# A residual block of two 3x3 convolutions: four operations of the inner planes change places on VectorE and ScalarE

## The chip, the cores and the metric

The kernel runs on one core of a Trainium2 chip. The metric is the device time in microseconds. Before the change the median of 3 runs is 612.59 us (612.04 to 614.04). A core has a matrix engine (TensorE, PE in the rows; its weight loads are PEld), VectorE (DVE), ScalarE (ACT), GpSimd (POOL) and SyncE (SP), each with a queue of its own that runs in order.

## The reference

The input x is 32 images of 64 channels, 56 x 56, in float32; w1 and w2 are 64 x 64 x 3 x 3.

```python
def _conv3x3(x, w, stride=1):
    return jax.lax.conv_general_dilated(x, w, window_strides=(stride, stride), padding=((1, 1), (1, 1)), ...)
def _bn(x, gamma, beta, mean, var):
    inv = gamma * jax.lax.rsqrt(var + EPS)
    return x * inv[None, :, None, None] + (beta - mean * inv)[None, :, None, None]
identity = x
out = jax.nn.relu(_bn(_conv3x3(x, w1, stride=1), g1, b1, m1, v1))
out = _bn(_conv3x3(out, w2, stride=1), g2, b2, m2, v2)
return jax.nn.relu(out + identity)
```

## The kernel before, in words

**Layout.** An image is split into four planes by the parity of row and column. The 128 partitions are 64 channels times the row parity; the column parity makes two planes per partition, "even" and "odd", of 28 rows by 28 columns.

**Transform.** Along a row each convolution of three taps is done for two neighbouring columns at once with four products instead of six: two "inner" ones, on the sum and on the difference of two planes, and two "outer" ones, on differences with a shift. The inner products go to the PSUM banks SUM_T1 and SUM_T2, the outer ones to EVEN and ODD. In between, a *join* on VectorE writes EVEN and ODD from SUM_T1 plus and minus SUM_T2, of which ScalarE has made two copies with the bias, z (*copy_sum*, L562 and L563). The outer products are added onto that. PSUM is used whole: two halves of an image (14 or 15 row pairs), each with its four banks, by both convolutions in turn.

**Precision.** Each transformed plane t goes to TensorE as hi plus lo: hi is t rounded (ScalarE, *high_x*, *high_hidden*), lo is t minus hi (VectorE, *split_x*, *split_hidden*). A product is three matmul passes, hi by w_hi, hi by w_lo and lo by w_hi, with two matmuls each for the two row offsets, so 12 for the two inner products of a half and 12 for the outer ones. An image takes 96.

**Names.** *sum_hidden*, *difference_hidden* (L427, L433) make the inner planes t_inner of conv 2 from `hidden`; *outer_hidden* (L441) makes t_outer. ti_hi and ti_lo are the rounded t_inner and its rest, h_hi and h_lo those of t_outer. There is one buffer of ti_hi and ti_lo. *residual* (L543) puts half of the input's inner planes into SUM_T1 and SUM_T2, so that conv 2's inner products add onto the identity. *relu_hidden* (L568) writes `hidden` from EVEN and ODD, *relu_out* (L591) writes out_sb, which SyncE stores.

**Steps.** All engines run the same steps s, written out by hand, in a loop of four steps a turn with some steps ahead and behind. In step s TensorE does: conv 1's inner products of image s and conv 2's outer products of image s-2, for half 0 and then for half 1 (48 matmuls); then conv 2's inner products of image s-1 and conv 1's outer products of image s, for half 0 and then half 1 (48 matmuls). The order on each engine is the order of the code; semaphores count the finished pieces. What matters here:

- join(1, s, 0) overwrites EVEN and ODD of half 0, and waits until relu_out(s-2, 0) has read them. relu_out(s-2, 0) waits for conv 2's outer products of half 0.
- join(2, s-2, 1) waits for relu_hidden(s-1, 1), and so does sum_hidden(s-1). TensorE's inner products of conv 1, half 1, wait for that join.
- high_hidden("inner", s-1) waits for both t_inner planes, split_hidden("inner", s-1) for ti_hi, and TensorE's inner products of conv 2 for ti_lo and for residual of their half.
- residual(s-1, 0) waits for join(1, s, 0), which has read SUM_T1 of that half.
- Step 0 and 1 have no relu_out or join of conv 2; the step after the last image is written apart, half by half.

```python
def join(conv, n, half, before):
    dve.wait_ge(z_ready[conv], 2 * n + half + 1)
    dve.wait_ge(inner[conv], 2 * (2 * n + half) + 2)
    wait(dve, *((hidden_ready if before[0] == 1 else out_ready), 2 * before[1] + half + 1))
```

Of the kernel before, what the change touches and what calls it, by code (L numbers as in the profile page):

```python
# [24 lines left out]
def residual_block(nc, x, w1, w2, params, out):  # L25
# [17 lines left out]
    with ExitStack() as ctx:  # L43
# [100 lines left out]
        def wait(eng, semaphore, value):  # L144

            if isinstance(value, int) and value <= 0:
                return
            eng.wait_ge(semaphore, value)
# [12 lines left out]
        def is_step(s, number):  # L161

            return isinstance(s, int) and s == number

        def there_is(s, image):

            return not isinstance(s, int) or 0 <= image < N
# [90 lines left out]
        def hidden_rows(half):  # L258

            return slice(0, NP) if half is None else slice(*HALF1[half])  # L260
# [101 lines left out]
        def _(dve):  # L362
# [58 lines left out]
            def sum_hidden(n, half=None):  # L421

                rows = hidden_rows(half)

                dve.wait_ge(hidden_ready, 2 * n + (2 if half is None else half + 1))
                wait(dve, hlo_ready["inner"], n)
                nc.vector.tensor_tensor(t_inner[:, 0, rows], hid_data[:, 0, rows, 0:WQ], hid_data[:, 1, rows, 0:WQ],  # L427
                                        ALU.add)

            def difference_hidden(n, half=None):  # L430

                rows = hidden_rows(half)
                nc.vector.tensor_tensor(t_inner[:, 1, rows], hid_data[:, 1, rows, 0:WQ], hid_data[:, 0, rows, 0:WQ],  # L433
                                        ALU.subtract).then_inc(th_ready["inner"], 1)
# [9 lines left out]
            def split_hidden(which, n, b, half=None):  # L444

                full, hi, lo = hidden_parts(which, b, half)

                dve.wait_ge(hhi_ready[which], n + 1 + (half or 0))
                nc.vector.tensor_tensor(lo, full, hi.bitcast(F32), ALU.subtract).then_inc(hlo_ready[which], 1)  # L449

            def step(s, k):
                ahead, now, last = there_is(s, s + 1), there_is(s, s), there_is(s, s - 1)
                ka, kl = (k + 1) % 4, (k + 3) % 4
                if is_step(s, N):

                    sum_hidden(N - 1, 0)
                    difference_hidden(N - 1, 0)
                    outer_hidden(N - 1, 0)
                    split_hidden("inner", N - 1, kl % 2, 0)
                    sum_hidden(N - 1, 1)  # L460
                    difference_hidden(N - 1, 1)
                    join(2, N - 2, 1, before_conv2(N - 2))
                    split_hidden("outer", N - 1, kl % 2, 0)
                    outer_hidden(N - 1, 1)
                    split_hidden("inner", N - 1, kl % 2, 1)
                    join(2, N - 1, 0, before_conv2(N - 1))
                    split_hidden("outer", N - 1, kl % 2, 1)
                    return

                if there_is(s, s - 2):  # L470
                    join(2, s - 2, 1, before_conv2(s - 2))
                if last:
                    sum_hidden(s - 1)
                    difference_hidden(s - 1)
                    outer_hidden(s - 1)
                if now:
                    join(1, s, 0, (2, s - 2))

                if last:
                    split_hidden("inner", s - 1, kl % 2)  # L480
                if ahead:
                    difference_x(s + 1, ka)
                if now:
                    join(1, s, 1, (2, s - 2))

                if ahead:
                    outer_x(s + 1, ka)
                if last:
                    split_hidden("outer", s - 1, kl % 2)
                if is_step(s, -1):  # L490
                    low_weights(dve, "inner1")
                if ahead:
                    split_x("inner", s + 1, ka)

                if last:
                    join(2, s - 1, 0, before_conv2(s - 1))
                if is_step(s, -1):
                    low_weights(dve, "outer1")
                if ahead:
                    split_x("outer", s + 1, ka)  # L500
# [4 lines left out]
        def _(act):  # L505
# [29 lines left out]
            def residual(n, k, half):  # L535

                j0, j1 = HALF2[half]
                width = (j1 - j0) * WQ

                before = before_conv2(n)  # L540
                act.wait_ge(joined[before[0]], 2 * before[1] + half + 1)
                for i, bank, share in ((0, SUM_T1, 0.5), (1, SUM_T2, -0.5)):
                    ins = nc.scalar.activation(psum[:, half, bank, 0:width].rearrange("p (j q) -> p j q", q=WQ),  # L543
                                               x_full("inner", k)[0][:, i, j0:j1], ACT.Copy, scale=share)
                ins.then_inc(res_ready, 1)
# [9 lines left out]
            def copy_sum(conv, n, half):  # L555

                r0, r1 = (HALF1, HALF2)[conv - 1][half]
                width = (r1 - r0) * WQ

                act.wait_ge(inner[conv], 2 * (2 * n + half) + 1)  # L560
                t2 = psum[:, half, SUM_T2, 0:width]
                nc.scalar.activation(z[:, half, 0, 0:width], t2, ACT.Identity, bias=bias[:, conv - 1:conv])  # L562
                nc.scalar.activation(z[:, half, 1, 0:width], t2, ACT.Identity, bias=bias[:, conv - 1:conv],  # L563
                                     scale=-1.0).then_inc(z_ready[conv], 1)
# [21 lines left out]
            def relu_out(n, half):  # L586
                j0, j1 = HALF2[half]

                act.wait_ge(outer[2], 2 * n + half + 1)
                wait(act, stored[half], 16 * n)  # L590
                nc.scalar.activation(out_sb[:, half], psum[:, half, EVEN:ODD + 1, 0:(j1 - j0) * WQ],  # L591
                                     ACT.Relu).then_inc(out_ready, 1)

            def step(s, k):
                ahead, now, last = there_is(s, s + 1), there_is(s, s), there_is(s, s - 1)
                ka, kl = (k + 1) % 4, (k + 3) % 4
                if is_step(s, N):

                    residual(N - 1, kl, 0)
                    high_hidden("inner", N - 1, kl % 2, 0)  # L600
                    relu_hidden(N - 1, 1)
                    high_hidden("outer", N - 1, kl % 2, 0)
                    relu_out(N - 2, 0)
                    copy_sum(2, N - 1, 0)
                    high_hidden("inner", N - 1, kl % 2, 1)
                    residual(N - 1, kl, 1)
                    high_hidden("outer", N - 1, kl % 2, 1)
                    relu_out(N - 2, 1)
                    copy_sum(2, N - 1, 1)
                    return  # L610
                if is_step(s, 0):

                    act.wait_ge(prep[2], 2)
                    act.wait_ge(outer_taps[2], 1)
                    act.wait_ge(mat_zeroed, 2)
                    fill_matrix(copy, "all2", HID_BLOCKS)

                    act.wait_ge(bias_ready, 1)
                    act.wait_ge(zeroed, 1)
                if last:  # L620
                    relu_hidden(s - 1, 1)
                if now:
                    copy_sum(1, s, 0)
                if last:
                    high_hidden("inner", s - 1, kl % 2)
                if there_is(s, s - 2):
                    relu_out(s - 2, 0)
                if now:
                    copy_sum(1, s, 1)
                if last:  # L630
                    residual(s - 1, kl, 0)
                if there_is(s, s - 2):
                    relu_out(s - 2, 1)
                if last:
                    high_hidden("outer", s - 1, kl % 2)
                    copy_sum(2, s - 1, 0)
                    residual(s - 1, kl, 1)
                if is_step(s, 0):
                    high_weights("all2")
                if ahead:  # L640
                    high_x("inner", s + 1, ka)
                if is_step(s, -1):
                    high_weights("outer1")
                if now:
                    relu_hidden(s, 0)
                if ahead:
                    high_x("outer", s + 1, ka)
                if last:
                    copy_sum(2, s - 1, 1)
# [132 lines left out]
```

## Time and profile before

| | |
|---|---|
| median of 3 runs | 612.59 us |
| profiled execution | 612.13 us, span 610.5 us |
| mean granted TensorE clock | 0.991 of full speed |
| TensorE matmul, weight load | 93%, 91% of the span |
| VectorE, ScalarE, GpSimd | 90%, 80%, 8% |
| DMA | 79.90 MB, mean 131 GB/s |

The busy shares are those of the engines' instructions. A row of a timeline gives the start from the span's beginning, the duration, the engine, the line, what is written and read, the shapes and how often; in brackets stands the idle time of the engine before it and what ended it. Instructions of one engine that run back to back overlap by about 0.1 us, so the distance of two starts, not the duration, is what one costs.

### The profile page before, as it was taken

To read this page: it belongs to the slowest core of one execution; us is meant where nothing else is said; L and a number is where in the kernel's file an instruction comes from. 1 tells how busy PE (TensorE), PEld (TensorE's weight loads), DVE (VectorE), ACT (ScalarE), POOL (GpSimd) and SP (SyncE) were. 2 spreads that over 40 slices of the span, in tenths; PEclk is the share of its full clock that TensorE was granted. 3 is DMA by queue.
4 is the path that set the end of the run, shared out by engine and by line. 5 is a ranking of instruction groups with operands and counts; after the bars stand their busy time and mean duration, and the time that the engine had idled before them with its cause. 6 is when DMAs were issued, how large, how long until landed. Compare 5 with 4: busy or idle time off the path is not lost.

```text
span 610.5 us, 8987 instructions
## 1 busy us (share of the span) xinstructions
PE 570.0 (93%) x3090; PEld 553.2 (91%) x3090; DVE 549.7 (90%) x443; ACT 487.7 (80%) x730; POOL 47.9 (8%) x52
## 2 busy tenths in 40 slices
PE   6769999999999999999999999999999999999997
PEld 3669999999999999999999999999999999999997
DVE  4699999999999999999999999999999999999974
ACT  4687789887788887787987778888778888778785
POOL 6700000000000000000000000000000000000000
PEclk9789999999999999999999999999999999999999
DMA  8444455435445444445443445534444534440112
GB/s 296 104 85 135 140 159 156 136 95 149 138 135 161 138 114 125 135 135 162 143 135 98 139 141 152 156 130 102 149 135 135 162 135 127 117 137 27 53 54 105
DMA packets 31679, 79.90 MB, mean 131 GB/s; under 512 B 2608, under 2 KB 19120, under 8 KB 31664
## 3 DMA queue, kind: packets, MB, share of 16 engines
q1 hardware_dynamic: 26912, 66.11, 29.9%
q0 software_dynamic: 4608, 13.31, 14.2%
q10 hardware_dynamic: 144, 0.29, 0.2%
q8 instruction: 9, 0.15, 0.1%
q14 instruction: 6, 0.05, 0.0%
HBM read 54.01 MB, written 25.69 MB: 131 GB/s over the span
## 4 chain that ended last, share of the span: by engine, by line
PE 56%; DVE 15%; issue 12%; ACT 12%; DMA 1%; POOL 0%; DVEq 0%; ACTq 0%
PE psum L669 56%; DVE ti_lo L449 9%; ACT out_sb L591 4%; DVE t_inner L433 3%; ACT hidden L568 3%; ACT z L563 2%; ACT z L562 2%; DVE t_inner L427 1%; ACT ti_hi L553 1%; DMA x_inner<-x_dram 1%; DVE psum L418 1%; ACT x_hi L533 0%; POOL w_mat L218 0%; DVE x_lo L404 0%; ACTq L560 0%
## 5 line engine op out<-in xcount | busy, mean ns | idle before, releaser
L669 PE MATMUL psum<-x_hi,w_hi 128*128 128x392 f32 (+2 forms) x512 | 176.3, 344 | 9.2 <-DVE x_lo L404 9.2
L669 PE MATMUL psum<-x_hi,w_lo 128*128 128x392 f32 (+2 forms) x512 | 175.5, 343 | 0.0
L669 PE MATMUL psum<-x_lo,w_hi 128*128 128x392 f32 (+2 forms) x512 | 175.3, 342 | 0.0
L418 DVE TENSOR_TENSOR psum<-psum,z 128x784 f32<-128x784 f32 (+1 forms) x128 | 127.1, 993 | 40.8 <-ACT hidden L568 14.4
L669 PE MATMUL psum<-ti_hi,w_hi 128*128 128x392 f32 x256 | 90.6, 354 | 23.8 <-DVE ti_lo L449 23.8
L669 PEld LDWEIGHTS psum<-x_hi,w_hi 128*128 128x128 f32 x512 | 97.4, 190 | 10.5 <-issue 6.3
L669 PEld LDWEIGHTS psum<-x_lo,w_hi 128*128 128x128 f32 x512 | 97.2, 190 | 0.4
L669 PEld LDWEIGHTS psum<-x_hi,w_lo 128*128 128x128 f32 x512 | 97.2, 190 | 0.4
L553 ACT ACTIVATE ti_hi<-t_inner 128x1624 fp32r<-128x1624 f32 (+2 forms) x33 | 50.3, 1524 | 54.2 <-DVE t_inner L433 54.2
L669 PE MATMUL psum<-h_hi,w_hi 128*128 128x392 f32 x256 | 87.2, 341 | 0.0
L669 PE MATMUL psum<-h_lo,w_hi 128*128 128x392 f32 x256 | 87.2, 341 | 0.0
L669 PE MATMUL psum<-ti_lo,w_hi 128*128 128x392 f32 x256 | 87.2, 341 | 0.0
L669 PE MATMUL psum<-ti_hi,w_lo 128*128 128x392 f32 x256 | 87.0, 340 | 0.0
L669 PE MATMUL psum<-h_hi,w_lo 128*128 128x392 f32 x256 | 86.9, 340 | 0.0
L568 ACT ACTIVATE hidden<-psum 64x56 f32<-64x56 f32 (+2 forms) x128 | 61.2, 504 | 29.6 <-PE psum L669 29.2
L562 ACT ACTIVATE z<-psum,bias 128x392 f32<-128x392 f32 (+1 forms) x128 | 75.1, 587 | 5.8 <-PE psum L669 2.7
L669 PEld LDWEIGHTS psum<-ti_hi,w_hi 128*128 128x128 f32 x256 | 48.0, 188 | 33.9 <-DVE ti_lo L449 24.8
L563 ACT ACTIVATE z<-psum,bias 128x392 f32<-128x392 f32 (+1 forms) x128 | 75.7, 592 | 0.0
L330 POOL DMA_DIRECT2D x_inner<-x_dram x32 | 28.1, 887 | 485.5 <-DMA x_inner<-x_dram 485.5
L543 ACT ACTIVATE psum<-x_inner 128x392 f32<-128x392 f32 x128 | 59.2, 501 | 7.1 <-DVE psum L418 7.1
L404 DVE TENSOR_TENSOR x_lo<-x_inner,x_hi 128x1568 fp32r<-128x1568 f32 x32 | 57.1, 1783 | 3.5 <-ACT x_hi L533 3.5
L591 ACT ACTIVATE out_sb<-psum 128x784 f32<-128x784 f32 x64 | 52.1, 814 | 9.4 <-PE psum L669 8.6
(66 smaller groups left out, 829.3 us busy)
## 6 DMA issues: line engine op xcount, KB each, us to landing
x_sb<-x_dram SPq DMA_DIRECT2D x32, 814.0 KB, 4.8
out_dram<-out_sb SPq DMA_DIRECT2D x64, 392.0 KB, 2.8
x_inner<-x_dram SPq DMA_DIRECT2D x32, 406.0 KB, 3.2
x_inner<-x_dram POOLq DMA_DIRECT2D x32, 406.0 KB, 5.1
z<-w_dram ACTq DMA_DIRECT2D x1, 288.0 KB, 3.8
out_sb<-w_dram SPq DMA_DIRECT2D x1, 288.0 KB, 6.2
bn<-params_dram SPq DMA_DIRECT2D x1, 132.0 KB, 3.6
```

What stands on the lines that cost most here:

```text
L330: pool.dma_start(x_inner[:, k, 0], odd, accum_op=ALU.add).then_inc(summed[k], 16)
L404: nc.vector.tensor_tensor(x_part(x_lo, k, places), full, x_part(x_hi, k, places).bitcast(F32), ALU.subtract).then_inc(xlo_ready[which], 1)
L418: nc.vector.tensor_tensor(psum[:, half, EVEN:ODD + 1, 0:width], t1, z[:, half, :, 0:width], ALU.add).then_inc(joined[conv], 1)
L433: nc.vector.tensor_tensor(t_inner[:, 1, rows], hid_data[:, 1, rows, 0:WQ], hid_data[:, 0, rows, 0:WQ], ALU.subtract).then_inc(th_ready["in ...
L449: nc.vector.tensor_tensor(lo, full, hi.bitcast(F32), ALU.subtract).then_inc(hlo_ready[which], 1)
L543: ins = nc.scalar.activation(psum[:, half, bank, 0:width].rearrange("p (j q) -> p j q", q=WQ), x_full("inner", k)[0][:, i, j0:j1], ACT.Cop ...
L553: nc.scalar.activation(hi, full, ACT.Copy).then_inc(hhi_ready[which], 1)
L562: nc.scalar.activation(z[:, half, 0, 0:width], t2, ACT.Identity, bias=bias[:, conv - 1:conv])
L563: nc.scalar.activation(z[:, half, 1, 0:width], t2, ACT.Identity, bias=bias[:, conv - 1:conv], scale=-1.0).then_inc(z_ready[conv], 1)
L568: return nc.scalar.activation(hid_data[rows, :, pairs, 0:WQ], sums[rows], ACT.Relu)
L591: nc.scalar.activation(out_sb[:, half], psum[:, half, EVEN:ODD + 1, 0:(j1 - j0) * WQ], ACT.Relu).then_inc(out_ready, 1)
L669: ins = nc.tensor.matmul(psum[:, half, bank, first:first + (j1 - j0) * WQ], w[:, i, far, :], moving, start=not onto and at == 0, stop=at = ...
```

## The change

Within a step, for images in the middle of the run: on VectorE sum_hidden(s-1) stands ahead of join(2, s-2, 1). On ScalarE relu_out(s-2, 0), the copy for the first store, stands ahead of high_hidden("inner", s-1), and residual(s-1, 0) ahead of copy_sum(1, s, 1). Nothing is added or taken away, and TensorE, SyncE and GpSimd have the order they had.

```diff
@@ the step of VectorE
+                if last:
+                    sum_hidden(s - 1)
                 if there_is(s, s - 2):
                     join(2, s - 2, 1, before_conv2(s - 2))
                 if last:
-                    sum_hidden(s - 1)
                     difference_hidden(s - 1)
                     outer_hidden(s - 1)
@@ the step of ScalarE
                 if now:
                     copy_sum(1, s, 0)
-                if last:
-                    high_hidden("inner", s - 1, kl % 2)
                 if there_is(s, s - 2):
                     relu_out(s - 2, 0)
+                if last:
+                    high_hidden("inner", s - 1, kl % 2)
+                    residual(s - 1, kl, 0)
                 if now:
                     copy_sum(1, s, 1)
-                if last:
-                    residual(s - 1, kl, 0)
                 if there_is(s, s - 2):
                     relu_out(s - 2, 1)
```

ScalarE, a step of the loop, before. L562 and L563 with 420 columns are copy_sum(1, s, 0), with 392 copy_sum(1, s, 1); ISA and REGISTER_ALU rows are waits and their counts.

```order
L563 ACTIVATE z<-psum,bias 128x420
L148 REGISTER_ALU
L553 ACTIVATE ti_hi<-t_inner 128x1624
L148 REGISTER_ALU
L591 ACTIVATE out_sb<-psum 128x784
L560 ISA
L562 ACTIVATE z<-psum,bias 128x392
L563 ACTIVATE z<-psum,bias 128x392
L543 ACTIVATE psum<-x_inner 128x392 x2
L591 ACTIVATE out_sb<-psum 128x784
```

The same step of ScalarE with the change:

```order
L563 ACTIVATE z<-psum,bias 128x420
L148 REGISTER_ALU
L591 ACTIVATE out_sb<-psum 128x784
L148 REGISTER_ALU
L553 ACTIVATE ti_hi<-t_inner 128x1624
L541 REGISTER_ALU
L543 ACTIVATE psum<-x_inner 128x392 x2
L560 ISA
L562 ACTIVATE z<-psum,bias 128x392
L563 ACTIVATE z<-psum,bias 128x392
L591 ACTIVATE out_sb<-psum 128x784
```

out_sb has moved one place up past ti_hi, and the residual's two writes past the two z copies.

VectorE, the beginning of a step of the loop, as a difference. The first L418 is join(2, s-2, 1), L427 is sum_hidden, L404 the last operation of the step before.

```order
 L404 TENSOR_TENSOR x_lo<-x_outer,x_hi 128x1568
-L414 ISA
-L418 TENSOR_TENSOR psum<-psum,z 128x2x392
-L427 TENSOR_TENSOR t_inner<-hidden 128x812
+L427 TENSOR_TENSOR t_inner<-hidden 128x812
+L414 ISA
+L418 TENSOR_TENSOR psum<-psum,z 128x2x392
 L433 TENSOR_TENSOR t_inner<-hidden 128x812
 L441 TENSOR_TENSOR t_outer<-hidden 128x1624
```

The join with its wait has moved one place down, behind the sum; the difference and what follows stand where they stood.

## Rows read from the trace of the kernel before

**Rows 1.** The page, busy time of each engine and TensorE's granted clock by slices.
```profile
PE 570.0 (93%) x3090; PEld 553.2 (91%) x3090; DVE 549.7 (90%) x443; ACT 487.7 (80%) x730; POOL 47.9 (8%) x52
...
PEclk9789999999999999999999999999999999999999
```

**Rows 2.** Waits: who waited for whom, us in total, times, longest.
```profile
ACT ti_hi L553 <- DVE t_inner L433: 54.2, 31, 1.8
...
PE psum L669 <- DVE ti_lo L449: 23.8, 31, 2.5
```

**Rows 3.** Groups by line and shape, VectorE's joins of conv 1, half 0.
```profile
L418 DVE TENSOR_TENSOR psum<-psum,z 128x840 f32<-128x840 f32 x32 | 33.3, 1041 | 23.0 <-PE psum L669 11.5 <-ACT out_sb L591 9.7 <-ACT z L563 1.9
```

**Rows 4.** Timeline of ScalarE in one step.
```profile
303.90 1.00 ACT L568 ACTIVATE hidden<-psum 64x56 f32<-64x56 f32 x2 [0.95 <-PE psum L669]
...
305.51 0.60 ACT L563 ACTIVATE z<-psum,bias 128x420 f32<-128x420 f32 x1
307.95 1.57 ACT L553 ACTIVATE ti_hi<-t_inner 128x1624 fp32r<-128x1624 f32 x1 [1.84 <-DVE t_inner L433]
309.42 0.80 ACT L591 ACTIVATE out_sb<-psum 128x784 f32<-128x784 f32 x1
310.12 0.58 ACT L562 ACTIVATE z<-psum,bias 128x392 f32<-128x392 f32 x1
...
312.46 0.82 ACT L591 ACTIVATE out_sb<-psum 128x784 f32<-128x784 f32 x1
...
314.62 0.58 ACT L562 ACTIVATE z<-psum,bias 128x392 f32<-128x392 f32 x1
...
315.56 0.93 ACT L543 ACTIVATE psum<-x_inner 128x392 f32<-128x392 f32 x2
316.41 1.51 ACT L533 ACTIVATE x_hi<-x_inner 128x1568 fp32r<-128x1568 f32 x1
...
320.53 0.57 ACT L563 ACTIVATE z<-psum,bias 128x392 f32<-128x392 f32 x1
```

**Rows 5.** Timeline of VectorE, that step, with the first and last regular sum_hidden.
```profile
52.25 1.00 DVE L427 TENSOR_TENSOR t_inner<-hidden 128x812 f32<-128x812 f32 x1
...
305.03 0.98 DVE L418 TENSOR_TENSOR psum<-psum,z 128x784 f32<-128x784 f32 x1 [0.50 <-ACT hidden L568]
305.92 0.99 DVE L427 TENSOR_TENSOR t_inner<-hidden 128x812 f32<-128x812 f32 x1
306.84 1.00 DVE L433 TENSOR_TENSOR t_inner<-hidden 128x812 f32<-128x812 f32 x1
307.75 1.84 DVE L441 TENSOR_TENSOR t_outer<-hidden 128x1624 f32<-128x1624 f32 x1
310.32 1.04 DVE L418 TENSOR_TENSOR psum<-psum,z 128x840 f32<-128x840 f32 x1 [0.73 <-PE psum L669]
311.27 1.84 DVE L449 TENSOR_TENSOR ti_lo<-t_inner,ti_hi 128x1624 fp32r<-128x1624 f32 x1
...
318.32 1.78 DVE L404 TENSOR_TENSOR x_lo<-x_inner,x_hi 128x1568 fp32r<-128x1568 f32 x1
...
320.91 1.78 DVE L404 TENSOR_TENSOR x_lo<-x_outer,x_hi 128x1568 fp32r<-128x1568 f32 x1
...
577.45 1.00 DVE L427 TENSOR_TENSOR t_inner<-hidden 128x812 f32<-128x812 f32 x1
```

**Rows 6.** Timeline of TensorE's matmuls in the same step.
```profile
303.70 0.35 PE L669 MATMUL psum<-x_hi,w_hi 128*128 128x420 f32 x1
...
307.87 0.34 PE L669 MATMUL psum<-h_lo,w_hi 128*128 128x392 f32 x1
...
312.08 0.34 PE L669 MATMUL psum<-h_lo,w_hi 128*128 128x392 f32 x1
...
321.85 0.35 PE L669 MATMUL psum<-x_hi,w_hi 128*128 128x420 f32 x1
```

**Rows 7.** Chain that ended last, in order of time: start us, us, what.
```profile
313.17 8.86 PE psum L669 x48
```

More of the change, by code:

```diff
@@ L623, in step @@
                     copy_sum(1, s, 0)
+                if there_is(s, s - 2):
+                    relu_out(s - 2, 0)
                 if last:
                     high_hidden("inner", s - 1, kl % 2)
-                if there_is(s, s - 2):
-                    relu_out(s - 2, 0)
+                    residual(s - 1, kl, 0)
                 if now:
                     copy_sum(1, s, 1)
-                if last:
-                    residual(s - 1, kl, 0)
                 if there_is(s, s - 2):
```

## The prediction, made before the changed kernel ran

> **What bounds the kernel now.** I read the busy shares first. TensorE is busy for 93% of the span and VectorE for 90%, at a granted clock of nine or ten tenths in every slice behind the first ones [rows 1]; so no engine is full, but two leave little. Then the waits, longest first. What TensorE waits for is one thing: the low part of the inner hidden planes, ti_lo, 31 times and 23.8 us in all. ScalarE waits longest (54.2 us) for the t_inner planes from which ti_hi comes. Both are in [rows 2]. VectorE's largest idle time, sorted by line and shape, is 23.0 us in front of the 32 joins of conv 1's first half, put down to PE, out_sb and z [rows 3].
>
> Then one step of the loop on three engines, the one in which s-1 is rounded from 308 us on [rows 4 to 6]. TensorE starts conv 1's inner products at 303.70 and would, at its own pace, be ready for conv 2's inner products at 312.26: the last matmul starts at 312.08, and the 48 matmuls up to it lie (312.08 - 303.70)/47 = 0.178 us apart. It starts them at 313.17. So 0.91 us of a step of 18.11 us is lost ((577.45 - 52.25)/29, from the first and the last regular sum_hidden [rows 5]). The reader should follow why, backwards: ti_lo (DVE, 311.27 to 313.11) stands behind join(1, s, 0), which begins at 310.32, although the operation before it ended at 309.59. That join may not overwrite the bank pair until relu_out(s-2, 0) has read it. relu_out ran at 309.42 to 310.22 [rows 4], because it stands behind high_hidden, which itself waited until 307.95 for the difference. Yet relu_out's own input was ready at 308.21 (307.87 + 0.34, the last matmul of outer 2 on half 0 [rows 6]). In the chain of waits one piece, 8.86 us of matmuls, goes from 313.17 to 322.03 [rows 7] and ends in the next relu_hidden(s, 1): up to there it is TensorE alone that decides, so a start that comes earlier moves everything after it.
>
> **ScalarE, part by part.** No instruction is added or taken away; 30 steps (s = 2 to 31) have all the moved pieces. Step 1 has no relu_out and no join of conv 2, and the last step is written apart and unchanged.
>
> relu_out(s-2, 0) moves ahead of high_hidden. It now waits for TensorE itself: 308.21 + 0.04 (the 0.04 is relu_out at 312.46 behind the matmul that ends at 312.42) = 308.25. The next instruction starts 0.70 later (309.42 to 310.12), so high_hidden starts at 308.95 instead of 307.95 and ends at 308.95 + 1.57 = 310.52. That is a cost of 1.00 us on ti_hi, and a gain of 1.17 us on out_sb.
>
> residual(s-1, 0) moves ahead of the two z copies of conv 1's half 1. It waits for join(1, s, 0), which on the new path (below) runs from 309.51 to 310.55; residual starts at about 310.6, and with its spacing of 0.85 (315.56 to 316.41, the other residual) the z copies begin at 311.44 and take 0.94 (314.62 to 315.56), up to 312.38. relu_out(s-2, 1) waits for TensorE at 312.46 [rows 4] as before. So this move costs nothing: cover is that wait, with 0.08 us to spare, and if it fails ScalarE is late by what is over, into a later slack of 0.27 us (below). TensorE needs residual by 312.5 and has it at 311.5. The z copies come 1.3 us later than before, and their reader join(1, s, 1) would be at 313.2 (behind ti_lo, from 310.6, and difference_x, 1.76 + 0.89 by the spacings of such operations), 0.7 us behind them.
>
> **VectorE.** sum_hidden and join(2, s-2, 1) change places. Both wait for the same relu_hidden, so sum starts at 305.03, the join 0.92 later (the spacing of sum, 305.92 to 306.84), and the difference at 306.84 as before [rows 5]. Only the join is later, by 0.92 us; it ends near 306.93. Behind it waits TensorE's inner product of conv 1, half 1, which follows the matmul of 307.87 [rows 6], at 308.05: 1.1 us of cover. The gain of this move alone is 0, its cost 0 as long as that cover holds. Its wait stands with the queue of VectorE behind it, but is over before VectorE comes to it.
>
> join(1, s, 0) no longer waits: out_sb is ready at 309.05, outer_hidden releases VectorE at 309.51 (307.75 + 1.84 less an overlap of 0.08), so it starts at 309.51 instead of 310.32, and ti_lo could start 0.95 later, at 310.46 (0.81 us gained). But ti_hi is ready only at 310.52; the row nearest to a wait of VectorE for ScalarE is 0.13 (join at 305.03 behind relu_hidden's end at 304.90), and ScalarE behind VectorE needs 0.11 (ti_hi at 307.95 behind the difference, which ends at 306.84 + 1.00); ScalarE behind TensorE needs 0.04. I take 0.08: ti_lo runs from 310.60 to 312.44, TensorE starts 0.06 later as now (313.11 to 313.17), at 312.50. **Gain of a step: 0.67 us.** Bounds: 0.81 if ti_hi does not decide, 0.55 if the wait costs more, as a register instruction comes between.
>
> **What is late next.** TensorE stands 0.24 us instead of 0.91 us; with no wait at all the gain would be 0.91. The rest of the step has to follow by 0.67. ScalarE after relu_out(s-2, 1) is unmoved: high_x for the inner planes ends at 316.41 + 1.51 = 317.92, its last z copy at 320.53 + 0.57 = 321.10; TensorE then releases relu_hidden near 322.04 - 0.67 = 321.37. It keeps 0.27 of the 0.95 us it idles there now [rows 4]. VectorE would reach x_lo at 318.32 - 0.67 = 317.65, waits for that high_x until about 318.00, and so is only 0.32 ahead; it ends its last split at 320.91 + 1.78 - 0.32 = 322.37, and sum is due at 321.37 + 1.13 = 322.50 (305.03 against 303.90) [rows 5]. So the idle 0.50 us in front of that place takes the wait, with 0.13 to spare. TensorE's next block waits for join(2, s-1, 0), which ends some 0.1 behind the start of the last split, at 321.0 - 0.32 = 320.7, and comes at 321.18 (321.85 - 0.67 [rows 6]). SyncE and the loads keep their order, and x_inner has whole steps of lead. The sum: 30 x 0.67 = 20.1 us.
>
> The spacing of matmuls deserves a doubt: relu_out now hangs on it, and the row gives 0.178 us. In the Trainium skill, "TensorE: Matmul & The Clock Gate", section "Back-to-back issue gap", the warm gap of an isolated matmul is N/2.4 + 2.5 ns, 0.166 us for 392 columns. By it relu_out's input would come some 0.2 us earlier, VectorE's own 0.81 would decide, and 24 us would be gained; the trace does not agree at full clock, and I go by the row.
>
> The profiled execution took 612.13 us at a span of 610.5, 0.46 under the median of 612.59. From its own time 612.13 - 20.1 = 592.0; from the median 592.5. I forecast **592.0 us**.
>
> **The rivals.**
> *Nearly all of TensorE's stand goes.* ti_hi is not late, and TensorE hardly stands at all. Gain 0.81 to 0.91, 24 to 27 us: 585 to 588 us. Against it speak ti_hi at 310.52 and VectorE's order; chance 12%.
> *The slack of 0.13 us on VectorE and 0.27 us on ScalarE is used up.* Both engines then go round at their own pace: VectorE's waits grow where ScalarE's high_x is late. The price is what is over, some 0.1 to 0.4 a step; gain 0.3 to 0.55: 596 to 603 us. For it: VectorE is at 90%, ScalarE has no gap from 311 to 321. Against: the spacings used are those of back-to-back rows. Chance 15%.
> *No change.* high_hidden's new wait for outer 2 eats all: if relu_out's input came at 308.92 rather than 308.21, ti_lo would be where it is. It would need TensorE's first 24 matmuls to be 0.7 us later than the row. Chance 4%: 611 to 614 us.
> *Slower.* The join of conv 2's half 1 becomes TensorE's wait. Its place: ahead of inner product 1, half 1. From the point where that join ends after 308.05 (1.1 us later than I have it), each microsecond stops TensorE, and since relu_out(s-2, 1) and the whole ScalarE row come behind, it is paid in full. It is a net loss once it exceeds 0.67, so with the join ending after 308.7; say 0.9: 30 x (0.9 - 0.67) = 7, 619 us. For it only that the join is now one place later, behind an operation of 0.91. Chance 4%.
>
> **How the numbers follow.** Forecast 65% (589 to 595.5), the larger gain 12%, the smaller 15%, none 4%, slower 4%. A change under 0.3% (1.8 us) is no change for this kernel, whose three runs lie 2.0 us apart. Faster: 65 + 12 + 15 = 92%; same 4%; slower 4%. The range takes in the forecast, half of the larger gain and the better half of the smaller: 586 to 600 us.
>
> **What would show it.** A step of about 17.44 us; TensorE's wait for ti_lo down from 0.7 to about 0.1 us each, some 5 us in all; ScalarE's 54 us of waiting for t_inner turned into about 2.1 us a step (306.11 to 308.25) of waiting for TensorE in front of out_sb; no idle time in front of the 840-wide join; a short wait of ti_lo for ti_hi; a new wait of about 0.3 us of x_lo for x_hi. It is wrong if the step is above 17.8 us, if TensorE waits for joins, or if relu_hidden starts late because ScalarE is still busy.

## The result and the profile after

The changed kernel takes 594.68 us (median of 4 runs, 594.67 to 595.89) against 612.39 us (612.04 to 614.04, 4 runs): ratio 0.9711, 95% interval 0.9689 to 0.9732, 17.7 us less. Forecast were 592.0 us, a range of 586 to 600, and 20.1 us. Of all executions of the kernel before, here and beside the experiments, one took 3157 us; it is left out of every ratio.

First the page of the changed kernel: busy time by engine, and the granted clock of TensorE. It answers to [rows 1].

```profile
PE 570.6 (96%) x3090; PEld 553.9 (93%) x3090; DVE 557.6 (94%) x443; ACT 485.4 (82%) x730; POOL 46.3 (8%) x52
...
PEclk9789999999999999999999999999999999999999
```

The work on each engine is nearly what it was; the span is shorter. The waits of the changed kernel (us in total, times, longest) answer to [rows 2]; line 669 of before is 668 now:

```profile
ACT out_sb L591 <- PE psum L668: 70.0, 33, 2.2
ACT hidden L568 <- PE psum L668: 13.1, 33, 1.4
...
PEld psum L668 <- DVE ti_lo L449: 10.2, 24, 0.5
...
DVE ti_lo L449 <- ACT ti_hi L553: 4.8, 25, 0.3
...
PE psum L668 <- DVE ti_lo L449: 3.9, 7, 2.7
...
ACT ti_hi L553 <- DVE t_inner L433: 0.5, 1, 0.5
```

ScalarE's 54.2 us in front of ti_hi are gone, and 70.0 us in front of out_sb have come; TensorE's 23.8 us for ti_lo are 3.9. This view counts TensorE's idle time from the modelled end of a matmul, 0.34 us behind its start, while the next one normally starts after 0.18 us; so it shows less than the stand that the distance of two starts gives, and below I use the distance. The groups by line and shape show the joins of [rows 3] without the 23.0 us of idle time, of which 1.9 are left:

```profile
L418 DVE TENSOR_TENSOR psum<-psum,z 128x840 f32<-128x840 f32 x32 | 33.1, 1035 | 1.9 <-ACT z L563 1.9
```

One step of the loop on the three engines. ScalarE, which answers to [rows 4]:

```profile
297.31 1.01 ACT L568 ACTIVATE hidden<-psum 64x56 f32<-64x56 f32 x2 [0.31 <-PE psum L668]
...
301.75 0.82 ACT L591 ACTIVATE out_sb<-psum 128x784 f32<-128x784 f32 x1 [2.22 <-PE psum L668]
302.47 1.55 ACT L553 ACTIVATE ti_hi<-t_inner 128x1624 fp32r<-128x1624 f32 x1
303.92 0.91 ACT L543 ACTIVATE psum<-x_inner 128x392 f32<-128x392 f32 x2
...
305.87 0.82 ACT L591 ACTIVATE out_sb<-psum 128x784 f32<-128x784 f32 x1
...
314.84 1.01 ACT L568 ACTIVATE hidden<-psum 64x56 f32<-64x56 f32 x2 [0.36 <-PE psum L668]
```

VectorE, which answers to [rows 5]:

```profile
298.35 1.00 DVE L427 TENSOR_TENSOR t_inner<-hidden 128x812 f32<-128x812 f32 x1
299.27 0.98 DVE L418 TENSOR_TENSOR psum<-psum,z 128x784 f32<-128x784 f32 x1
...
302.83 1.03 DVE L418 TENSOR_TENSOR psum<-psum,z 128x840 f32<-128x840 f32 x1
304.05 1.85 DVE L449 TENSOR_TENSOR ti_lo<-t_inner,ti_hi 128x1624 fp32r<-128x1624 f32 x1 [0.19 <-ACT ti_hi L553]
305.82 0.97 DVE L389 TENSOR_TENSOR x_inner<-x_sb 128x784 f32<-128x784 f32 x1
306.80 0.98 DVE L418 TENSOR_TENSOR psum<-psum,z 128x784 f32<-128x784 f32 x1
```

TensorE, which answers to [rows 6]:

```profile
301.29 0.34 PE L668 MATMUL psum<-h_lo,w_hi 128*128 128x392 f32 x1
...
305.49 0.34 PE L668 MATMUL psum<-h_lo,w_hi 128*128 128x392 f32 x1
305.96 0.45 PE L668 MATMUL psum<-ti_hi,w_hi 128*128 128x392 f32 x1
```

The reader should see the order of events: relu_out now starts 0.12 us behind the end of TensorE's last outer matmul of half 0 (301.63), the 840-wide join comes at once behind outer_hidden, and ti_lo waits 0.19 us for ti_hi, which ends at 304.02. TensorE would go on at 305.67 (305.49 + 0.18) and goes on at 305.96, so it stands 0.29 us instead of 0.91. The step is 314.84 - 297.31 = 17.53 us.

The mean step in the 24 steps of the loop, from the starts of outer_hidden, is 17.53 us (18.11 before); in the five behind it, which are written out, 17.43 us (18.09 before). TensorE's stand in front of its first matmul with ti_hi, taken in every step as the distance from the matmul before it less 0.18 us, adds up over the 30 steps to 26.2 us before and 8.4 us after. The difference, 17.7 us, is the whole gain. In the mean of the 24 steps of the loop it is 0.87 us before and 0.29 after; in the written-out ones it is 0.86 and 0.20.

The profiled execution is the longest of the four, 595.89 us (span 594.2). It lost its extra time ahead of the steady part. The stretch from 36 to 50 us, before and then after (length, then busy time of PE, PEld, DVE, ACT and POOL, the granted clock, the DMA share and GB/s):

```profile
36.00:50.00 14.00, 11.54 (x64) 11.25 (x63) 14.00 (x12) 11.66 (x17) 0.86 (x1) 0.97 0.32 102
```

```profile
36.00:50.00 14.00, 11.35 (x56) 11.01 (x55) 13.36 (x11) 10.96 (x16) 0.87 (x1) 0.88 0.32 112
```

A granted clock of 0.88 instead of 0.97 there (full is 2.4 GHz, the other level 1.2) gave eight matmuls less. The first regular difference_hidden, which has the same place in both orders, comes at 54.66 us instead of 53.16, so 1.5 us later. (The first sums, at 52.85 and at 52.25 [rows 5], are not the same place: before, a join stands ahead of the sum.) The kernel of experiment 1 that leaves residual where it was has VectorE's new order too. Its profiled execution took 594.28 us, had a granted clock of 1.00 from 40 to 48 us and its first difference_hidden at 52.96. Here the clock was 0.84 from 40 to 44 us and 0.73 from 44 to 48, and in the second of these, with TensorE busy throughout in both profiles, it did 18 matmuls against 24. So one execution can be 1.2 to 1.6 us longer than another by its start alone, and I compare steps and medians, not spans. Why the clock fell there is not known.

### The profile page after: what moved, and what is told of

The parts are those of the page before. It is cut to its first block, busy times and chain, and to the rows that moved or that the text cites. A ratio compares the mean times of both kernels' runs of the same rounds, so it can differ in the third digit from the quotient of the medians.

```text
span 594.2 us, 9017 instructions
## 1 busy us (share of the span) xinstructions
PE 570.6 (96%) x3090; PEld 553.9 (93%) x3090; DVE 557.6 (94%) x443; ACT 485.4 (82%) x730; POOL 46.3 (8%) x52
## 4 chain that ended last, share of the span: by engine, by line
PE 73%; DVE 10%; ACT 8%; issue 4%; DMA 1%; POOL 0%; ACTq 0%
PE psum L668 73%; DVE ti_lo L449 9%; ACT ti_hi L553 7%; DMA x_inner<-x_dram 1%; ACT x_hi L533 0%; ACT out_sb L591 0%; POOL w_mat L218 0%; DVE t_outer L441 0%; DVE x_lo L404 0%; POOL out_sb L191 0%; ACTq L148 0%; DVE t_inner L427 0%; ACTq L541 0%; DVE t_inner L433 0%; ACT hidden L568 0%
## 5 line engine op out<-in xcount | busy, mean ns | idle before, releaser
L418 DVE TENSOR_TENSOR psum<-psum,z 128x784 f32<-128x784 f32 (+1 forms) x128 | 127.0, 992 | 6.4 <-ACT z L563 2.7
L562 ACT ACTIVATE z<-psum,bias 128x392 f32<-128x392 f32 (+1 forms) x128 | 75.1, 587 | 4.9 <-PE psum L668 1.9
L563 ACT ACTIVATE z<-psum,bias 128x392 f32<-128x392 f32 (+1 forms) x128 | 75.7, 591 | 0.0
L449 DVE TENSOR_TENSOR ti_lo<-t_inner,ti_hi 128x1624 fp32r<-128x1624 f32 (+2 forms) x33 | 59.3, 1798 | 5.5 <-ACT ti_hi L553 4.8
L396 DVE TENSOR_TENSOR x_outer<-x_sb 128x1624 f32<-128x1624 f32 x32 | 61.0, 1907 | 0.0
L404 DVE TENSOR_TENSOR x_lo<-x_inner,x_hi 128x1568 fp32r<-128x1568 f32 x32 | 57.4, 1792 | 3.9 <-ACT x_hi L533 1.6
```

The costliest lines, as they stand in the source:

```text
L396: nc.vector.tensor_tensor(x_outer[:], runs(cells, 0, XPLANE), runs(cells, 1, XPLANE), ALU.subtract).then_inc(tx_ready["outer"], 1)
L404: nc.vector.tensor_tensor(x_part(x_lo, k, places), full, x_part(x_hi, k, places).bitcast(F32), ALU.subtract).then_inc(xlo_ready[which], 1)
L418: nc.vector.tensor_tensor(psum[:, half, EVEN:ODD + 1, 0:width], t1, z[:, half, :, 0:width], ALU.add).then_inc(joined[conv], 1)
```

## The experiments

In all of them the output is computed in full. Where a kernel has a few lines more or less, its line numbers are shifted by these. Each ratio is against the kernel before as it ran beside that experiment, with medians of 612.39 us (experiment 1), 612.50 (2 and 3) and 613.60 (4).

**1. Which of the three moves carries it.** Three kernels with one move or two.

Only relu_out:

```diff
+                if there_is(s, s - 2):
+                    relu_out(s - 2, 0)
                 if last:
                     high_hidden("inner", s - 1, kl % 2)
-                if there_is(s, s - 2):
-                    relu_out(s - 2, 0)
```

> Only relu_out(s-2, 0) goes ahead of high_hidden; sum_hidden and residual stay where they were before. Theory (the whole gain comes from the store copy that no longer stands behind the rounding): 594.7 us, a step of 17.5 us, residual behind the z copies ends 0.2 us before TensorE needs it. Rival (the sum ahead of the join, or the early residual, carries a part): 598 to 605 us.

Measured: 594.89 us (594.34 to 595.90), ratio 0.9711 (0.9697 to 0.9726); the step is 17.54 us. This one move carries the whole result.

The change without the move of residual:

```diff
 # against the changed kernel
                     high_hidden("inner", s - 1, kl % 2)
-                    residual(s - 1, kl, 0)
                 if now:
                     copy_sum(1, s, 1)
+                if last:
+                    residual(s - 1, kl, 0)
```

> The change without the move of residual: relu_out and sum_hidden are moved. Theory: residual ends at about 305.8 in the step that has TensorE's start at 305.96, so it does not decide: 594.7 us. Rival (TensorE now waits for residual instead of ti_lo): 0.1 to 0.3 us a step, 597 to 604 us.

Measured: 595.91 us (594.28 to 595.95), ratio 0.9722 (0.9708 to 0.9736), step 17.54 us. The median is 1.2 us above the changed kernel's; both kernels have runs near 594.5 and near 595.9, the steps are equal, and the intervals overlap. The move of residual is worth nothing that these runs show.

Only residual:

```diff
 # against the kernel before
+                if last:
+                    residual(s - 1, kl, 0)
                 if now:
                     copy_sum(1, s, 1)
-                if last:
-                    residual(s - 1, kl, 0)
```

> Only residual(s-1, 0) goes ahead of the z copies of conv 1, half 1. Theory: it waits for join(1, s, 0), which ends at 311.36 in the step shown, so ScalarE's row from there on is 0.7 us later, which its 0.95 us of idle time before relu_hidden takes up: 612.4 us, with idle time there down to about 0.2 us. Rival (the shift reaches TensorE through x_hi, x_lo or relu_hidden): 0.1 to 0.7 us a step, 615 to 633 us.

Measured: 612.23 us (611.98 to 613.96), ratio 0.9996 (0.9985 to 1.0006), step 18.12 us. ScalarE's timeline shows both halves of the argument:

```profile
311.37 0.92 ACT L543 ACTIVATE psum<-x_inner 128x392 f32<-128x392 f32 x2 [1.18 <-DVE psum L418]
...
313.17 0.83 ACT L591 ACTIVATE out_sb<-psum 128x784 f32<-128x784 f32 x1
...
322.02 1.01 ACT L568 ACTIVATE hidden<-psum 64x56 f32<-64x56 f32 x2 [0.24 <-PE psum L669]
```

residual waits 1.18 us for the join, the second out_sb comes 0.7 us later than in [rows 4], and the idle time before relu_hidden is 0.24 instead of 0.95 us. A wait was added, and slack took it.

Only the sum ahead of the join:

```diff
+                if last:
+                    sum_hidden(s - 1)
                 if there_is(s, s - 2):
                     join(2, s - 2, 1, before_conv2(s - 2))
                 if last:
-                    sum_hidden(s - 1)
                     difference_hidden(s - 1)
```

> Only sum_hidden goes ahead of join(2, s-2, 1). Theory: the difference comes when it came, the join has 1.1 us of cover, so nothing moves: 612.4 us (612.0 to 612.8). Rival (the sum carries a part of the gain, because hidden planes are read earlier): 600 to 609 us.

Measured: 609.94 us (609.65 to 611.34), ratio 0.9962 (0.9947 to 0.9977), step 18.04 instead of 18.11. The theory was wrong by 2.5 us: alone, this move gains. ScalarE's row and VectorE's:

```profile
303.21 1.00 ACT L569 ACTIVATE hidden<-psum 64x56 f32<-64x56 f32 x2 [0.87 <-PE psum L670]
```

```profile
304.25 1.00 DVE L427 TENSOR_TENSOR t_inner<-hidden 128x812 f32<-128x812 f32 x1 [0.39 <-ACT hidden L569]
305.17 0.98 DVE L418 TENSOR_TENSOR psum<-psum,z 128x784 f32<-128x784 f32 x1
```

sum_hidden starts 0.04 us behind relu_hidden's end (304.21); the join in its place started 0.13 us behind it [rows 4, 5], and 30 x 0.09 = 2.7 us is about what was gained. Written out, with no count in a register (experiment 3), the join still starts 0.14 us behind and the sum 0.03, so registers are not the reason. The join waits for three semaphores and has an instruction of its own for one of them (L414 in the order above); the sum waits for two. That this makes the difference is my reading and not shown: the join also differs in reading PSUM. In the changed kernel the gain is not seen (17.53 us a step, against 17.54 with relu_out moved alone), since there ti_hi decides and not VectorE's order.

**2. How much room the join has, and what it costs when it has none.** In the changed kernel the join of conv 2, half 1, goes one place further down, and then two.

```diff
                 if last:
                     sum_hidden(s - 1)
+                    difference_hidden(s - 1)
                 if there_is(s, s - 2):
                     join(2, s - 2, 1, before_conv2(s - 2))
                 if last:
-                    difference_hidden(s - 1)
                     outer_hidden(s - 1)
```

> The changed kernel with join(2, s-2, 1) one place further down, behind difference_hidden. It ends near 301.2 in the step in which TensorE's inner product of half 1 comes at 301.47. Theory: 0.3 us of cover are left and ti_hi is held by relu_out's wait for TensorE, not by the difference, so nothing moves: 594.7 us. Rival (the earlier difference lets ti_hi start earlier): 585 to 590 us; rival (the join's end reaches TensorE with its wait): 597 to 604 us.

Measured: 595.08 us (594.24 to 595.59), ratio 0.9710 (0.9694 to 0.9726), step 17.54 us: nothing moves, in either direction.

```diff
                 if last:
                     sum_hidden(s - 1)
+                    difference_hidden(s - 1)
+                    outer_hidden(s - 1)
                 if there_is(s, s - 2):
                     join(2, s - 2, 1, before_conv2(s - 2))
-                if last:
-                    difference_hidden(s - 1)
-                    outer_hidden(s - 1)
```

> The changed kernel with join(2, s-2, 1) behind outer_hidden: it ends near 302.95, 1.5 us after TensorE wants its bank pair. Theory (the mechanism of the slower rival: a late join is paid in full less TensorE's stand of 0.29 us): 30 x 1.2 to 1.3 = 36 to 39 us more, 631 to 634 us. Rival (TensorE's stand in front of ti_lo and other slack take up most): under 610 us.

Measured: 638.97 us (638.2 to 639.8), ratio 1.0428 (1.0411 to 1.0446), step 18.98 us, 1.45 more than in the changed kernel. Its waits:

```profile
DVE psum L418 <- ACT out_sb L590: 54.6, 30, 2.8
PE psum L667 <- DVE psum L418: 45.5, 30, 1.6
```

One step on TensorE:

```profile
301.04 0.34 PE L667 MATMUL psum<-h_lo,w_hi 128*128 128x392 f32 x1
302.96 0.42 PE L667 MATMUL psum<-x_hi,w_hi 128*128 128x392 f32 x1 [1.58 <-DVE psum L418]
```

By the distance of starts TensorE now stands 1.74 us here (1.68 in the mean), and in front of ti_hi it no longer stands at all. So 1.7 us have come and 0.3 have gone, and a late join is paid in full, as the mechanism says. The price is 0.2 us a step above what I expected. Most of that is that VectorE cannot follow: its sum starts 1.70 us behind the start of the last split, which is back to back, and so only 2.79 us ahead of the last outer matmul of half 0, where the changed kernel has 2.94. Two places down, the same operation goes from free to 44 us.

**3. The register instructions.** Both kernels with all steps written out, so that no wait takes its count from a register:

```diff
-            for s in (-1, 0, 1):
-                step(s, s % 4)
-            with eng.Fori(0, (N - 8) // 4) as turn:
-                for k in range(4):
-                    step(turn * 4 + (2 + k), (2 + k) % 4)
-            for s in range(N - 6, N + 2):
+            for s in range(-1, N + 2):
                 step(s, s % 4)
```

> The kernel before with all 34 steps written out, so that no wait has its count in a register. Theory (register instructions on ScalarE cost only where the wait behind them ends the chain, which is not so before): the last steps of before already take 18.09 against 18.12 us in the loop, 24 x 0.03 = 0.7 us less, 611.7 us. Rival (every step gets shorter by as much as in the changed kernel): 610 us.

Measured: 612.95 us (612.32 to 614.69), ratio 1.0005 (0.9995 to 1.0016), step 18.11 us. No gain, not even the 0.7 us.

> The changed kernel with all 34 steps written out. Theory (what the forecast of 0.67 a step missed, 0.08, is the register instructions between TensorE's end and relu_out, which only the 24 steps in the loop have): those steps come to the 17.43 us of the last steps, 24 x 0.10 = 2.4 us less, 592.3 us. Rival (the missing part lies in the moved work itself): 594.7 us.

Measured: 592.75 us (592.41 to 594.24), ratio 0.9676 (0.9662 to 0.9691), 1.9 us less than the changed kernel with its loop, and the mean step takes 17.44 us. The spans differ by 2.4 us (medians 593.0 and 590.6): both kernels with written-out steps have some 0.4 us more between span and time. TensorE's last outer matmul of half 0, and ScalarE's relu_out behind it:

```profile
315.70 0.34 PE L663 MATMUL psum<-h_lo,w_hi 128*128 128x392 f32 x1
```

```profile
316.08 0.83 ACT L586 ACTIVATE out_sb<-psum 128x784 f32<-128x784 f32 x1 [2.14 <-PE psum L663]
```

relu_out starts 0.04 us behind the matmul's end (316.04), against 0.12 in the loop (301.75 behind 301.63). In the loop a register instruction stands ahead of relu_out (the rows of the order in the section on the change show it); written out, the count is a constant. TensorE's stand falls from 0.28 us in three steps of a turn and 0.36 in the fourth to 0.20 in all, so it is not the jump at the turn's end alone. In the kernel before, the same instruction lay beside other waiting and cost nothing.

**4. If ti_hi decides, taking it off the path must gain.** Rounding is split: the plane of the sum is rounded while ScalarE waits for TensorE, the plane of the difference behind relu_out.

```diff
 # ScalarE's step
+                if last:
+                    high_sum(s - 1)            # ti_hi[:, 0] from t_inner[:, 0]
                 if there_is(s, s - 2):
                     relu_out(s - 2, 0)
                 if last:
-                    high_hidden("inner", s - 1, kl % 2)
+                    high_difference(s - 1)     # ti_hi[:, 1] from t_inner[:, 1]
                     residual(s - 1, kl, 0)
```

> The changed kernel with the rounding of ti in two instructions: the sum's plane in the 2.2 us in which ScalarE waits for TensorE ahead of relu_out(s-2, 0), the difference's plane behind relu_out. Theory (ti_hi behind relu_out's wait decides the step): ti_hi is ready 0.7 us earlier, VectorE's own order decides 0.24 us earlier than now, less up to 0.1 us of slack that the rest of the step does not have: 0.15 to 0.24 us a step, 588 to 590.5 us, and no more waiting of ti_lo for ti_hi. Rival (TensorE or VectorE is already at its pace): 594.7 us; rival (the 0.1 us of the added instruction reaches relu_hidden): 596 us or more.

Measured: 587.67 us (587.48 to 589.22), against 613.6 us of the kernel before in that session; ratio 0.9588 (0.9571 to 0.9606), step 17.29 us, 0.24 less than in the changed kernel. It has the lowest median of all, 7 us below the changed kernel. VectorE's and ScalarE's rows:

```profile
298.24 1.03 DVE L418 TENSOR_TENSOR psum<-psum,z 128x840 f32<-128x840 f32 x1
299.18 1.83 DVE L449 TENSOR_TENSOR ti_lo<-t_inner,ti_hi 128x1624 fp32r<-128x1624 f32 x1
...
302.12 0.98 DVE L418 TENSOR_TENSOR psum<-psum,z 128x784 f32<-128x784 f32 x1 [0.22 <-ACT out_sb L600]
```

```profile
297.07 0.83 ACT L600 ACTIVATE out_sb<-psum 128x784 f32<-128x784 f32 x1 [1.30 <-PE psum L679]
297.79 0.87 ACT L562 ACTIVATE ti_hi<-t_inner 128x812 fp32r<-128x812 f32 x1
```

ti_hi ends at 298.66, before the join ahead of ti_lo does, and ti_lo follows that join without a wait. TensorE's stand is 0.05 us in the mean. VectorE then has no slack left in front of its sum, which in nearly every step starts 1.70 to 1.77 us behind the start of the last split, which is back to back.

With the join ahead of the sum again, everything else as in the kernel of two roundings:

> As the kernel with two roundings of ti, but join(2, s-2, 1) ahead of sum_hidden again, as before the change. Theory (the join starts 0.09 us later behind relu_hidden than the sum does, and this counts only where VectorE's order decides): 0.09 x 30 = 2.7 us more than the kernel with two roundings and the sum first. Rival (the order of the two is of no account): the same time as that kernel.

Measured: 588.68 us (588.53 to 590.04), ratio 0.9610 (0.9593 to 0.9627). The step is 17.32 us in the loop and 17.35 behind it, where the kernel with the sum first has 17.29 and 17.27. So the direction holds and the size holds only in the written-out steps (0.09 us); in the loop it is a third of that. The intervals of the ratios overlap a little, so 1.0 us is a measurement of the steps rather than of the times.

> Two roundings of ti, the sum first, all 34 steps written out. Theory (registers cost on the path through relu_out, which no longer decides): little more than the looped kernel with two roundings, 0 to 1.5 us less. Rival (register instructions cost 0.1 us a step wherever they stand): 2.4 us less. It would be the fastest version either way, 586 to 590 us.

Measured: 588.12 us (587.89 to 589.20), ratio 0.9598 (0.9582 to 0.9614), step 17.28 us. No gain: the median spans are 586.0 us for both, so where relu_out does not decide, the form of its wait costs nothing. The rival is out, and that the written-out version would be the fastest was not borne out.

## Why the prediction was right, and where it was off

**What bounds.** Right: TensorE waited for ti_lo, which stood behind a join, which waited for relu_out, which stood behind the rounding. Moving relu_out alone gives the whole gain (experiment 1).

**relu_out ahead of high_hidden.** Right in mechanism: ScalarE's wait of 1.8 us for t_inner became one of 2.2 us for TensorE (2.1 forecast), and the 840-wide join no longer waits. The term of 0.67 us a step was mis-sized. It measured 0.58 in the 24 steps of the loop (18.11 to 17.53) and 0.66 in the written-out ones (18.09 to 17.43). It was 0.91 less 0.24 us of TensorE's stand; in the loop it is 0.87 less 0.29. The 0.91 was read in one step and taken for all, and it is among the longest (0.82 to 0.92). The 0.24 is too small because of "308.21 + 0.04": the 0.04 was read at relu_out of half 1, which has no register instruction ahead of it, while relu_out of half 0 has one and starts 0.12 behind. I read it off the wrong twin although the order showed the row. Of these 0.08 us, 0.05 came back at ti_hi (below), and 0.02 more went into small differences of the row. Written out, the kernel has the forecast's 17.44, but that is in part luck: the stand before was 0.04 us less than the 0.91 I used, and the stand left, 0.20, is 0.04 less than my 0.24.

**The wait of ti_lo for ti_hi.** Right that ti_hi decides: a wait of 0.19 us in the mean of the loop, and taking ti_hi off the path gains 0.24 us a step. The latency behind ti_hi, which I took as 0.08, is 0.03. The bounds of 0.55 and 0.81 held both sizes, and splitting the rounding brought the step to 0.82 below before, the upper end.

**residual ahead of the z copies.** Right: worth nothing, alone or with the others, and covered by the waits named.

**sum_hidden ahead of the join.** Half right. In this change it adds nothing, as forecast; but "the gain of this move alone is 0" failed: it is 2.5 us, because I gave both operations the same start behind relu_hidden, while the join's was 0.13 and the sum's 0.04 us behind it.

**What is late next.** ScalarE idles 0.31 and 0.36 us before relu_hidden (0.27 forecast). VectorE's sum starts 1.86 us behind the start of the last split in the step shown, and 1.86 to 2.00 in the loop, where back to back is 1.70. So it has 0.16 us of slack or more; 0.13 was forecast. The forecast wait of x_lo for x_hi is there, at half its size: 0.17 us (1.93 instead of 1.76 between the starts of the two splits), where 0.35 was worked out. One wait was missed: join(1, s, 1) waits for relu_out(s-2, 1), not only for its z copies. relu_out ends at 306.69 and the join starts at 306.80, 0.98 behind difference_x instead of 0.89. It costs nothing here; with a late join of conv 2 it grows to 54.6 us in all (experiment 2).

**The rivals.** The slower one was put in the right place: its mechanism costs 1.45 us a step once TensorE has to stand 1.7 us for the join, but this change stays clear of it, and even one place more was free. "Slack used up" (596 to 603 us) did not come: neither VectorE nor ScalarE lost its slack. The measured 594.7 lies near it for the two reasons given under relu_out, and these are no loss of slack. That TensorE hardly stands (585 to 588 us) needs the split rounding. By the isolated gap in the Trainium skill, "TensorE: Matmul & The Clock Gate", section "Back-to-back issue gap", an estimate of 0.166 us, relu_out would have come earlier and 24 us been gained. The traces do not agree: matmuls of 392 columns keep to 0.18 us in the changed kernel too, and relu_out came later, not earlier.

## What to carry to other kernels

When an engine waits for a chain of other engines, look in it for an operation that was ready long ago and only stood behind another in its own queue: here one such copy for a store was worth 17.7 us, and nothing else of the change anything. An operation moved ahead may wait itself; what then stands behind it can often be cut, and the part whose input is there already goes into that wait. Before a latency is read from a twin, compare what stands in the order ahead of both: here such differences were worth 0.08 to 0.09 us a step on the deciding chain and nothing beside it. And before one step is taken for all, read the same distance in several: the stand of TensorE was 0.82 to 0.92 us, and the step shown was near the top.

## What I had not expected of the hardware

Behind relu_hidden's end a join with three waits starts 0.13 us later, a sum with two 0.04 us; what in the join makes the difference is open. relu_out starts 0.12 us behind the matmul in the loop, with a register instruction ahead of it, and 0.04 us with the steps written out.

A matmul can cost 0.1 us more though it starts on time. The weight load of a matmul usually starts 0.18 us ahead of it. Where the load itself waits, both start together, the matmul takes 0.45 instead of 0.34 us, and the next starts 0.28 instead of 0.18 us behind it. This is so in front of ti_hi in both kernels, and also in steps of experiment 4's first kernel in which TensorE does not stand (the matmul before starts at 283.59):

```profile
283.76 0.19 PEld L679 LDWEIGHTS psum<-ti_hi,w_hi 128*128 128x128 f32 x1 [0.15 <-DVE ti_lo L449]
```

```profile
283.77 0.45 PE L679 MATMUL psum<-ti_hi,w_hi 128*128 128x392 f32 x1
```

The start of the kernel is not the same in each execution: with a granted clock of 0.84 and 0.73 in the two stretches from 40 to 48 us, the changed kernel took 595.89 us, 1.2 more than its median, which is more than some of the differences looked for here. The clock's mean from 36 to 50 us does not tell this alone. In the profile of experiment 1 with only the sum moved it was 0.88 too, but low from 36 to 40 us (0.57), where TensorE was waiting for part of the time in the other profiles, and 1.00 from 40 us on; that execution, 610.12 us, lies near its median of 609.94.
